# Layer 1's attention in a two-layer transformer kernel: projections cut in halves, transposes and softmax pieces moved between batches

## The chip, the cores and the metric

The kernel runs on one core of one Trainium2 chip, as one program with five instruction queues: TensorE (PE), VectorE (DVE), ScalarE (ACT), GpSimd (POOL) and SyncE (SP, which issues DMAs here). Each queue is executed in its own order, and semaphores tie them together. The metric is device time in microseconds; less is better.

## The reference, cut to what matters

Two layers run over x of 16 batches of 128 tokens, 128 wide. A layer is attention, then a feed-forward part. The change touches the first attention:

```
xn = layernorm(x) * g_norm                        # 16 batches x 128 tokens x 128
q  = l2norm((xn @ Wq) per head) * q_scale         # 16 heads of 64: 1024 columns
k, v = split(xn @ Wkv)                            # ONE key/value head of 64 for all 16 heads
k  = l2norm(k) * k_scale                          # null key and null value from cond_64 stand in front
sim = 8 * q @ k.T + relative position bias        # rel_pos_bias: a small MLP over distances
attn = softmax(causal and key mask(sim))          # 16 heads x 128 x 129
out = layernorm((attn @ v) @ Wout) * g_out
x  = x + ternary_ffn(out)                         # then layer 2: attention and an 8-expert top-2 MoE
```

The second attention has no l2norm of q and k; it ends in a router that chooses two of eight experts for every token, and those run last.

## The kernel before, in words

**Tiling.** One batch (128 tokens) is a step of a loop of 16. The 128 query rows of a batch are cut into four *units* u = 0..3 of 32 queries. A tile of scores has 128 partitions (4 head groups x 32 queries) and, for four such groups, 33, 65, 97 or 129 keys by unit: the causal mask lets later units see more keys. So a batch has four units of four pieces. Everything is fp32.

**The steps of a batch b, by their names in the code.** `input_norm` (DVE) normalises x; `turn_input` (PE) transposes it to psA, `input_T` (ACT) copies it out. `project_in` (PE, L761 to L777) multiplies it with Wkv (to psA) and with Wq in two halves h = 0, 1 of 512 columns (to the two banks of psQ). For the norm of q and k, `squares` (ACT, L1107 to L1113) squares both, `sum_squares` (DVE, L1416) adds up per head, POOL's `q_norm` (L584 to L590) takes a floor (L588) and a power -1/2 (L562), and `queries_norm` (DVE, L1421) multiplies. `turn_queries` (PE, L796) transposes the normed queries half by half back into psQ, `queries` (ACT, L1124) copies them to qT. `keys_in`, `turn_keys`, `keys_T` do the same for the keys.
Then, unit by unit: `scores` (PE, L810) to psS; `biased` (DVE, L1430) adds the bias that POOL's `mask_bias` (L613) has made and takes the row's maximum; `weights` (ACT, L1143) is the exponential with its sum; `divide` (DVE, L1438, L1442) normalises; `turn_pair` (units 0 and 1, L817) and `turn_probs` (units 2 and 3, L828) transpose; `pair_T` and `weights_T` (ACT, L1150, L1156) copy; `values_pair` and `values` (PE, L836, L846) multiply with v; `outputs` (DVE, L1451) reads; `project` (PE, L865) multiplies with Wout; `out_stats` and `out_centred` (DVE) start the output's norm. The value matrices of `values_pair` are spread to other partitions by six SP DMAs per batch (L478, L481), which wait for `values_set` (POOL, L596).

**What sets the order.** It is written out by hand: each engine's block has a function `batch(b, i)` that `over` calls, some first and last batches unrolled and the rest in a hardware loop of two. The two attentions share these functions, with `if layer == ...` where they differ. Work of neighbouring batches is interleaved: in batch b, PE also transposes and multiplies units 2 and 3 of b-1, projects Wout for b-2 and projects the input of b+2; ACT, DVE and POOL prepare q and k of b+1. psS has room for one unit of scores, so a unit's `scores` waits until DVE has read the one before; psQ holds both halves of one batch's q, so `project_in` of a batch waits until ACT has copied both transposed halves of the batch before (semaphore q_ready, raised once per batch).
POOL has one more duty in batches 3, 14 and 15 of the first layer: `hide` (L580) puts the causal mask into the second layer's bias table with 4, 6 and 6 instructions.

## Time and profile before

| | us |
|---|---|
| median of 3 runs | 679.77 (673.1, 679.77, 679.88) |
| the profiled execution's own time | 673.8 |
| its span | 672.1 |
| first attention, first scores to last projection | 55.8 to 278.9 |
| second attention's loop begins | about 336 |
| busy: PE, DVE, ACT, POOL | 493.2, 426.6, 378.4, 322.8 |

The span is what the profiler's records cover; the time adds what lies around it. Busy is the time in which an engine has an instruction in work; matmuls are pipelined and their ends are modelled. In a row of the timeline, the first number is the start from the span's beginning, the second the duration, and brackets tell how long the engine had been idle and on whose work it waited ("issue": for nothing that the profile shows). A line number is that of the kernel before.

### The profile page before, as it was taken

Reading aid. Unit: us, or ns where it says so; the run is one execution under the profiler, and the core shown is the slowest. Engines: PE = TensorE matmul, PEld = TensorE weight load, DVE = VectorE, ACT = ScalarE, POOL = GpSimd, SP = SyncE. Lnnn points to the kernel's source line nnn. Section 1 sums busy time; section 2 is a strip of 40 time slices with the busy share of each in tenths; the row PEclk is TensorE's granted clock in tenths of the full one; section 3 lists DMA queues with packets and bytes.
Section 4 is the critical chain, followed back from the end, with each engine's and each line's share of the span. In section 5 each row is a group of like instructions: output and inputs, shape, how many; then the busy total and the mean of one; then the engine's idle time right before and its main releaser. Section 6 shows DMA issues by size and latency. Waiting matters only on the chain.

```text
span 672.1 us, 13998 instructions
## 1 busy us (share of the span) xinstructions
PE 493.2 (73%) x3209; PEld 397.8 (59%) x3209; DVE 426.6 (63%) x2098; ACT 378.4 (56%) x1473; POOL 322.8 (48%) x397
## 2 busy tenths in 40 slices
PE   1057788888788887888679899999886505999930
PEld 0034566666566655756668787787775403887820
DVE  2644788778877888446367989888997421344313
ACT  1036876777677767465178787878685101444310
POOL 5235476446654683176343434252347660345660
PEclk9986999999999998999679999999999855999975
DMA  3822075220000000000000000000001112344316
GB/s 102 213 61 74 13 133 109 68 64 9 4 6 6 4 6 4 1 1 1 4 5 9 6 8 5 6 6 5 7 18 44 35 44 50 103 116 124 88 38 193
DMA packets 53757, 30.14 MB, mean 45 GB/s; under 512 B 19994, under 2 KB 50131, under 8 KB 53715
## 3 DMA queue, kind: packets, MB, share of 16 engines
q1 hardware_dynamic: 51154, 24.77, 15.7%
q0 software_dynamic: 2560, 4.90, 2.3%
q8 instruction: 15, 0.25, 0.2%
q14 instruction: 28, 0.22, 0.1%
HBM read 16.13 MB, written 11.42 MB: 41 GB/s over the span
## 4 chain that ended last, share of the span: by engine, by line
PE 39%; DVE 18%; issue 14%; SPq 10%; ACT 7%; DMA 6%; POOL 5%; DVEq 1%; POOLq 0%; ACTq 0%
PE psS L810 5%; PE psS L1061 5%; PE psQ L782 4%; DVE sc L1430 4%; DMA slot_rows<-Y,dest_u 4%; PE psQ L777 3%; PE psQ L1051 3%; PE psO L846 3%; ACT sc L1143 2%; SPq L448 2%; ACT qT L1124 2%; PE psA L865 2%; DVE centred L1494 2%; SPq L431 2%; DVE OT L1451 2%
## 5 line engine op out<-in xcount | busy, mean ns | idle before, releaser
L1143 ACT ACTIVATE sc<-sc,negmax 128x97 f32<-128x97 f32 (+3 forms) x512 | 179.2, 355 | 55.3 <-DVE negmax L1430 55.1
L1430 DVE CUSTOM_DVE_ANT_0 sc<-psS,wide_buf 128x97 f32<-128x97 f32 (+3 forms) x512 | 93.7, 239 | 65.2 <-PE psS L810 64.2
L810 PE MATMUL psS<-kk,qT 128*128 128x194 f32 (+3 forms) x512 | 102.7, 323 | 17.9 <-DVE negmax L1430 17.8
L613 POOL TENSOR_TENSOR wide_buf<-bias,mask 128x132 f32<-128x132 f32 (+3 forms) x128 | 104.3, 841 | 6.1 <-DVE negmax L1430 4.2
L810 PEld LDWEIGHTS psS<-kk,qT 128*128 128x128 f32 x512 | 81.1, 194 | 34.6 <-issue 30.7
L1143 ACT ACTIVATION_READ_ACCUMULATOR sc<-sc,negmax 128x1 f32 x512 | 97.8, 191 | 0.0
L1442 DVE TENSOR_TENSOR pn<-sc,rsum 128x128 f32<-128x128 f32 (+3 forms) x128 | 71.5, 559 | 8.7
L865 PE MATMUL psA<-Wo,OT 128*128 128x128 f32 (+1 forms) x512 | 65.5, 282 | 1.7 <-DVE OT L1451 1.7
L865 PEld LDWEIGHTS psA<-Wo,OT 128*128 128x128 f32 x512 | 62.9, 196 | 3.0 <-DVE OT L1451 2.6
L562 POOL TENSOR_TENSOR qrn<-qssc,half 128x9 f32<-128x9 f32 (+1 forms) x32 | 57.3, 1789 | 2.7
L588 POOL TENSOR_SCALAR qssc<-qss 128x9 f32<-128x9 f32 (+1 forms) x32 | 13.0, 405 | 91.8 <-DVE qss L1416 91.8
L1156 ACT COPY PT<-psT 96x512 f32<-96x512 f32 x64 | 37.4, 584 | 26.9 <-PE psT L828 26.0
L1451 DVE TENSOR_SCALAR OT<-psO,cols 128x512 f32<-128x512 f32 x64 | 47.7, 746 | 5.7 <-PE psO L846 3.9
L828 PE MATMUL psT<-ident,pn 128*96 128x128 f32 (+1 forms) x256 | 40.1, 280 | 14.8 <-issue 14.0
L1430 DVE DVE_READ_ACCUMULATOR2_ANT negmax<- 128x1 f32 x512 | 42.1, 82 | 0.0
L711 POOL DMA_INDIRECT choice_rows<-hT,tags x24 | 22.5, 939 | 39.7 <-ACT hT L1262 23.5
L828 PEld LDWEIGHTS psT<-ident,pn 128*96 128x96 f32 (+1 forms) x256 | 28.3, 140 | 19.9 <-issue 19.5
L846 PE MATMUL psO<-PT,vp 96*64 96x256 f32 (+1 forms) x256 | 34.8, 390 | 6.9 <-DVE OT L1451 5.3
L1061 PE MATMUL psS<-eW,hm 128*128 128x128 f32 x320 | 37.7, 277 | 2.7 <-DVE hm L1761 1.8
L625 POOL DMA_INDIRECT slot_rows<-Y,dest_u x32 | 31.3, 980 | 16.5 <-DMA slot_rows<-Y,dest_u 9.6
L1061 PEld LDWEIGHTS psS<-eW,hm 128*128 128x128 f32 x320 | 36.3, 192 | 4.8 <-issue 2.9
L596 POOL TENSOR_TENSOR vp<-kvs,vnull 128x64 f32<-128x64 f32 x32 | 13.1, 411 | 53.6 <-PE psO L846 53.6
(256 smaller groups left out, 1022.2 us busy)
## 6 DMA issues: line engine op xcount, KB each, us to landing
eW<-in_L_ffn_W SPq DMA_DIRECT2D x16, 256.0 KB, 3.0
slot_rows<-empty SPq DMA_DIRECT2D x2, 1390.0 KB, 11.7
xb<-slot_rows SPq DMA_DIRECT2D x16, 139.0 KB
vp_u<-vp SPq DMA_DIRECT2D x128, 8.0 KB
choice_rows<-zero_row SPq DMA_DIRECT2D x8, 256.0 KB, 3.0
wide_buf<-choice_rows SPq DMA_DIRECT2D x8, 256.0 KB, 4.5
Wq<-in_L_cond_Wq SPq DMA_DIRECT2D x2, 512.0 KB, 6.9
vp_u<-vp SPq DMA_DIRECT2D x64, 16.0 KB
```

The lines of the kernel that those rows point to most:

```text
L562: pool.tensor_tensor(dst, src, half[:, 0:k], ALU.pow).then_inc(done, count)
L613: pool.tensor_tensor(unit_masked(i, u).rearrange("p h e k -> p (h e) k"), unit_bias(layer, u).rearrange("p h e k -> p (h e) k"), mask[laye ...
L810: m = pe.matmul(psS[:, h, 0:2 * w], qT[i][:, h, u].rearrange("p m q -> p (m q)"), kk[i][:, :, 0:w], start=True, stop=True)
L828: m = pe.transpose(psT[0:k, probs_bank(u, i), g * P:(g + 1) * P], pn[u][:, g, :], ident[:])
L846: m = pe.matmul(psO[DH * e:DH * (e + 1), 2 * P * (u - 2):2 * P * (u - 1)], vp[i][0:k, :], PT[u - 1][0:k, :, e, :], start=True, stop=True)
L865: m = pe.matmul(psA[:, Y_AT[layer]:4 * P], OT[i][:, j].rearrange("p u q -> p (u q)"), Wo[layer][:, j, :], start=(j == 0), stop=(j == 7))
L1061: m = pe.matmul(psS[:, c, n * P:(n + 1) * P], hm[:, j, t * P:(t + 1) * P], eW2[i][:, j, :], start=(j == 0), stop=(j == FB - 1))
L1143: m = act.activation(v, v, ACT.Exp, bias=negmax[:, u, g:g + 1], scale=-1.0, accum_out=psum_row[:, u, g:g + 1])
L1156: act.copy(PT[u - 1][0:k].rearrange("p h e q -> p (h e q)"), psT[0:k, probs_bank(u, i), :]).then_inc(s["probsT_ready"], 1)
L1430: dve.tensor_tensor_reduce(sc[u][:, h, e, :], unit_psum(u)[:, h, e, :], unit_masked(i, u)[:, h, e, :], -1.0, -FAR, ALU.add, ALU.min, accum ...
L1442: dve.tensor_tensor(pn[u][:], sc[u][:].rearrange("p h e k -> p (h e) k")[:, :, 1:k + 1], rsum[:, u, :].unsqueeze(2).broadcast_to([P, 4, k] ...
L1451: dve.tensor_scalar(OT[i][:, :, 2 * half_of:2 * half_of + 2, :], psO[:].rearrange("p (u j q) -> p j u q", u=2, q=QB), cols[:, C_VN:C_VN + ...
```

## The change

The first layer's attention gets a function of its own on each engine (`attention_first`); the second layer's keeps the old order (`attention_second`). No arithmetic is added or taken away.

* **PE:** `project_in` is cut into `project_values` and `project_heads(b, h)`. The projection of b+1 (before: of b+2, at the end of b) now stands at the beginning of batch b: the k/v part and half 0 ahead of the first scores, half 1 behind them. `turn_queries` is cut as well: half 0 of b+1 comes at the end of batch b after its last scores, half 1 is the first thing of batch b+1. In the last batch's tail `project` of 14 goes ahead of `values_pair` of 15.
* **ACT:** q_ready rises per half. The copy of the queries (`queries`) moves to the beginning of their own batch; the exponentials of unit 3 of b-1, and their copy PT, move from the end of b-1 into batch b. `squares` is cut, its second half goes behind unit 0's exponentials.
* **DVE:** unit 3's `biased` of b-1 moves into batch b, with `divide` of unit 2. The statistics of the output are spread, so that none waits for the one just before it.
* **POOL:** floor and power of each half are apart from each other, with mask additions in between; the power of half 1 becomes the first instruction of the next batch. `values_set` of batch b moves from the end of b-1 to the beginning of b, and `hide` from the beginning of a batch to its end.
* **Second layer:** its two projection halves wait for q_ready one by one.

The core of the diff. The context is the new functions; lines that only moved into `attention_second` with `layer == 1` resolved are left out, and so are the removed lines, which the kernel above shows.

```diff
@@ POOL
+NORMS = ((0, 9), (9, HEADS + 1))
+def q_floored(b, h):
+    lo, hi = NORMS[h]
+    apart(pool, (s["ss_step"], 2 * b + h + 1))
+    pool.tensor_scalar(qssc[:, lo:hi], qss[:, lo:hi], 1e-24, None, ALU.max).then_inc(s["q_floor"], 1)
+def q_rsqrt(b, h):
+    lo, hi = NORMS[h]
+    pool.wait_ge(s["q_floor"], 2 * b + h + 1)
+    rsqrt(qrn[:, lo:hi], qssc[:, lo:hi], hi - lo, s["rn_ready"])
...
+def attention_first():
     def batch(b, i):
+        first, last = no(b, 0), no(b, NB - 1)
+        if not first:
+            q_rsqrt(b, 1)
+            values_set(0, b, i)
+        if not last:
+            mask_bias(0, b + 1, 0, 1 - i)
+            mask_bias(0, b + 1, 1, 1 - i)
+            q_floored(b + 1, 0)
+            mask_bias(0, b + 1, 2, 1 - i)
+            q_rsqrt(b + 1, 0)
+            mask_bias(0, b + 1, 3, 1 - i)
+            q_floored(b + 1, 1)
+        if isinstance(b, int) and b in (3, NB - 2, NB - 1):
             hide(b)
+    q_floored(0, 0)
+    q_rsqrt(0, 0)
+    q_floored(0, 1)
+    q_rsqrt(0, 1)
+    values_set(0, 0, 0)
+    pool.wait_ge(rel_in, 16 * 32)
+    pool.wait_ge(s["masks_ready"], 1)
+    for u in range(UNITS):
+        mask_bias(0, 0, u, 0)
+    over(pool, NB, batch, 4, 2)
+    for g in range(QUADS - 1):
+        dense_rstd(g)
...
@@ PE
+def project_values(b, i):
+    pe.wait_ge(s["xnT_ready"], b + 1)
+    held(pe, s["kk_ready"], b)
+    pe.matmul(psA[:, P:2 * P], xnT[i][:], Wkv[0][:], start=True, stop=True).then_inc(s["kv_psum"], 1)
+def project_heads(b, h, i):
+    held(pe, s["q_ready"], 2 * b + h - 1)
+    pe.matmul(psQ[:, h, :], xnT[i][:], Wq[0][:, 512 * h:512 * (h + 1)],
+              start=True, stop=True).then_inc(s["q_psum"], 1)
+def project_in(b, i):
+    B = b + NB
     pe.wait_ge(s["xnT_ready"], B + 1)
+    pe.matmul(psA[:, V_AT[1]:V_AT[1] + DH], xnT[i][:], Wkv[1][:, DH:P], start=True,
+              stop=True).then_inc(s["kv_psum"], 1)
+    pe.matmul(psA[:, KT_AT[1]:KT_AT[1] + P], Wkk[:].rearrange("p a d -> p (a d)"), xnT[i][:],
+              start=True, stop=True).then_inc(s["kT_psum"], 1)
+    if no(b, NB - 1):
         pe.wait_ge(s["r_pos_read"], 1)
+    for h in range(2):
+        pe.wait_ge(s["q_ready"], 2 * B + h - 1)
+        for j in range(4):
+            m = pe.matmul(psQ[:, h, j * P:(j + 1) * P], Wq[1][:, (4 * h + j) * P:(4 * h + j + 1) * P],
+                          xnT[i][:], start=True, stop=True)
+        m.then_inc(s["q_psum"], 1)
 def turn_keys(b, i):
     pe.wait_ge(s["k_ready"], b + 1)
     pe.transpose(psA[:, 2 * P:3 * P], kd[i][:].rearrange("p a d -> p (a d)"), ident[:]).then_inc(
         s["kT_psum"], 1)
+def turn_queries(b, h):
+    pe.wait_ge(s["qn_ready"], 2 * b + h + 1)
+    for j in range(4):
+        m = pe.transpose(psQ[:, h, j * P:(j + 1) * P], qn[:, (4 * h + j) * P:(4 * h + j + 1) * P],
+                         ident[:])
+    m.then_inc(s["qT_psum"], 1)
...
+def attention_first():
     def batch(b, i):
         first, last = no(b, 0), no(b, NB - 1)
+        turn_queries(b, 1)
+        if not last:
+            project_values(b + 1, 1 - i)
+            project_heads(b + 1, 0, 1 - i)
+        if not first:
+            turn_probs(b - 1, 2, 1 - i)
+        scores(0, b, 0, i)
+        if not first:
+            values_pair(b - 1, 1 - i)
+        if not last:
+            project_heads(b + 1, 1, 1 - i)
+        scores(0, b, 1, i)
+        if not first:
+            turn_probs(b - 1, 3, 1 - i)
+        if not first and not no(b, 1):
+            project(0, b - 2, i, not last)
+        scores(0, b, 2, i)
+        if not first:
+            values(b - 1, 1 - i)
+        scores(0, b, 3, i)
+        if not last and not no(b, NB - 2):
+            turn_input(0, b + 2, i)
+        if not last:
+            turn_keys(b + 1, 1 - i)
+            turn_queries(b + 1, 0)
+        turn_pair(b, i)
+    pe.wait_ge(attw_in, 16 * 8)
+    turn_input(0, 0, 0)
+    project_values(0, 0)
+    project_heads(0, 0, 0)
+    project_heads(0, 1, 0)
+    turn_input(0, 1, 1)
+    turn_keys(0, 0)
+    turn_queries(0, 0)
+    turn_ternary()
+    over(pe, NB, batch, 2, 2)
+    turn_probs(NB - 1, 2, 1)
+    project(0, NB - 2, 0, False)
+    values_pair(NB - 1, 1)
+    gate_rows_T()
+    turn_probs(NB - 1, 3, 1)
+    values(NB - 1, 1)
+    project(0, NB - 1, 1, False)
...
@@ ACT
+    if layer == 0:
+        held(act, s["kT_psum"], B)
     held(act, s["q_psum"], 2 * B - 2)
     c = C_GN0 if layer == 0 else C_GIN1
     act.activation(xnT[i][:], psA[:, 0:P], ACT.Copy, scale=cols[:, c:c + 1]).then_inc(
         s["xnT_ready"], 1)
+def squares(b, h):
     held(act, s["ss_step"], 2 * b)
+    if h == 0:
+        act.wait_ge(s["kv_psum"], b + 1)
+        act.activation(qsq[:, 0, :], psA[:, P:P + DH], ACT.Square)
+    act.wait_ge(s["q_psum"], 2 * b + h + 1)
+    act.activation(qsq[:, 1 + 8 * h:9 + 8 * h, :], psQ[:, h, :].rearrange("p (h d) -> p h d", d=DH),
+                   ACT.Square).then_inc(s["sq_ready"], 1)
 def queries(layer, b, i):
     B = b + NB * layer
             act.wait_ge(s["qT_psum"], 2 * b + h + 1)
         else:
             act.wait_ge(s["q_psum"], 2 * B + h + 1)
+        act.activation(qT[i][:, h].rearrange("p u m q -> p m u q"),
+                       psQ[:, h, :].rearrange("p (m u q) -> p m u q", u=UNITS, q=QB), ACT.Copy,
+                       scale=1.0 if layer == 0 else DH ** -0.5).then_inc(s["q_ready"], 1)
...
+def attention_first():
     def batch(b, i):
+        first, last = no(b, 0), no(b, NB - 1)
+        queries(0, b, i)
+        if not first:
+            pair_T(b - 1, 1 - i)
+        if not last:
+            squares(b + 1, 0)
+        if not first:
+            weights(4 * (b - 1) + 3, 3)
+            weights_T(b - 1, 2, 1 - i)
+        weights(4 * b, 0)
+        if not last:
+            squares(b + 1, 1)
+        if not first:
+            weights_T(b - 1, 3, 1 - i)
+        weights(4 * b + 1, 1)
+        weights(4 * b + 2, 2)
+        if not last and not no(b, NB - 2):
+            input_T(0, b + 2, i)
+        if not last:
+            keys_T(0, b + 1, 1 - i)
+    act.wait_ge(s["cols_ready"], 1)
+    input_T(0, 0, 0)
+    squares(0, 0)
+    squares(0, 1)
+    keys_T(0, 0, 0)
+    input_T(0, 1, 1)
+    ternary_T()
+    over(act, NB, batch, 2, 2)
+    pair_T(NB - 1, 1)
+    weights(4 * NB - 1, 3)
+    weights_T(NB - 1, 2, 1)
+    down_scaled()
+    gate_WoT()
+    weights_T(NB - 1, 3, 1)
...
@@ DVE
+def attention_first():
     def batch(b, i):
+        n = 4 * b
+        first, last = no(b, 0), no(b, NB - 1)
+        reads = not first and not no(b, 1)
+        queries_norm(b, 1)
+        if not first:
+            divide(b - 1, 2)
+        if reads:
+            outputs(b - 2, 1, i)
+        if not first:
+            biased(n - 1, 3, 1 - i)
+        if not last and not no(b, NB - 2):
+            input_norm(0, b + 2, i)
+        if not last:
+            sum_squares(b + 1, 0)
+            values_in(0, b + 1, 1 - i)
+        biased(n, 0, i)
+        if not first:
+            divide(b - 1, 3)
+            outputs(b - 1, 0, 1 - i)
+        biased(n + 1, 1, i)
+        divide(b, 0)
+        if not last:
+            queries_norm(b + 1, 0)
+            sum_squares(b + 1, 1)
+        else:
+            dense_stats(0)
+        if reads:
+            out_stats(0, b - 2, i)
+        biased(n + 2, 2, i)
+        if reads:
+            moments(b - 2, i)
+        if not last:
+            keys_in(b + 1, 1 - i)
+        else:
+            dense_stats(1)
+        if reads:
+            out_centred(b - 2, i)
+        divide(b, 1)
+    input_norm(0, 0, 0)
+    input_norm(0, 1, 1)
+    ternary()
+    values_in(0, 0, 0)
+    sum_squares(0, 0)
+    sum_squares(0, 1)
+    keys_in(0, 0)
+    queries_norm(0, 0)
+    over(dve, NB, batch, 4, 2)
+    divide(NB - 1, 2)
+    outputs(NB - 2, 1, 0)
+    biased(4 * NB - 1, 3, 1)
+    f_norm_in(0)
+    divide(NB - 1, 3)
+    outputs(NB - 1, 0, 1)
+    out_stats(0, NB - 2, 0)
+    moments(NB - 2, 0)
+    gate_rows_in()
+    out_centred(NB - 2, 0)
+    outputs(NB - 1, 1, 1)
+    f_norm_in(1)
+    dense_stats(2)
+    out_stats(0, NB - 1, 1)
+    moments(NB - 1, 1)
+    out_centred(NB - 1, 1)
...
```

The order on **PE** in a loop batch, before. The rows go from the last scores of a batch (L810, 258 columns) to the third piece of the next one:

```order
L796 MATMUL psQ<-ident,qn 128x128 x3
L340 ISA
L810 MATMUL psS<-kk,qT 128x258 [waits scores_ready,const_done]
L810 MATMUL psS<-kk,qT 128x258
L340 ISA
L817 MATMUL psT<-ident,pn 128x128 [waits probsT_ready,probs_ready,const_done]
L819 MATMUL psT<-ident,pn 128x128 x2
L767 MATMUL psA<-Wkv,xnT 128x128 [waits q_ready,xnT_ready]
L777 MATMUL psQ<-Wq,xnT 128x512 x2
L340 ISA
L810 MATMUL psS<-kk,qT 128x66 [waits q_ready,scores_ready,kk_ready,const_done]
```

and in the changed kernel, from the same place (L830 is `scores`, L816 `turn_queries`, L782 and L787 the projections, L848 `turn_probs`):

```order
L816 MATMUL psQ<-ident,qn 128x128 [waits qn_ready]
L816 MATMUL psQ<-ident,qn 128x128 x3
L782 MATMUL psA<-Wkv,xnT 128x128 [waits kk_ready,xnT_ready]
L787 MATMUL psQ<-Wq,xnT 128x512 [waits q_ready]
L848 MATMUL psT<-ident,pn 96x128 [waits probsT_ready,probs_ready,const_done]
L848 MATMUL psT<-ident,pn 96x128 x3
L340 ISA
L830 MATMUL psS<-kk,qT 128x66 [waits q_ready,scores_ready,kk_ready,const_done]
L830 MATMUL psS<-kk,qT 128x66
```

Between the last scores of a batch and the first of the next PE had both halves of the projection; now it has one half, the second half's transposes, and a piece of the batch before.

The order on **POOL** in batch 3, before (L613 `mask_bias`, L588 floor, L562 power, L596 `values_set`, L580 `hide`):

```order
L580 AFFINE_SELECT bias<-bias 32x4x32 x4
L613 TENSOR_TENSOR wide_buf<-bias,mask 128x132
L588 TENSOR_SCALAR qssc<-qss 128x9
L562 TENSOR_TENSOR qrn<-qssc,half 128x9
L588 TENSOR_SCALAR qssc<-qss 128x8
L562 TENSOR_TENSOR qrn<-qssc,half 128x8
L613 TENSOR_TENSOR wide_buf<-bias,mask 128x260
L613 TENSOR_TENSOR wide_buf<-bias,mask 128x388
L613 TENSOR_TENSOR wide_buf<-bias,mask 128x516
L596 TENSOR_TENSOR vp<-kvs,vnull 128x64
```

and in the changed kernel, batch 3 and the first instruction of batch 4 (L617 `mask_bias`, L589 floor, L600 `values_set`):

```order
L562 TENSOR_TENSOR qrn<-qssc,half 128x8
L600 TENSOR_TENSOR vp<-kvs,vnull 128x64
L617 TENSOR_TENSOR wide_buf<-bias,mask 128x132
L617 TENSOR_TENSOR wide_buf<-bias,mask 128x260
L589 TENSOR_SCALAR qssc<-qss 128x9
L617 TENSOR_TENSOR wide_buf<-bias,mask 128x388
L562 TENSOR_TENSOR qrn<-qssc,half 128x9
L617 TENSOR_TENSOR wide_buf<-bias,mask 128x516
L589 TENSOR_SCALAR qssc<-qss 128x8
L580 AFFINE_SELECT bias<-bias 32x4x32 x4
```

The power of half 1 now stands behind the batch's end, so in batches 3 and 14 `hide` stands between that half's floor and its power.

The order on **DVE** at the end of a loop batch in the changed kernel (L1508, L1512 `divide`, L1491 `queries_norm`, L1521 `outputs`, L1500 `biased`):

```order
L1512 TENSOR_TENSOR pn<-sc,rsum 128x256 [waits probsT_psum,rsum_ready]
L1491 TENSOR_TENSOR qn<-psQ,qrn 128x512 [waits qT_psum,rn_ready]
L1508 RECIPROCAL rsum<-psum_row 128x4 [waits exp_done]
L334 REGISTER_ALU [waits rsum_ready]
L1512 TENSOR_TENSOR pn<-sc,rsum 128x384 [waits probsT_psum]
L1518 REGISTER_ALU
L1521 TENSOR_SCALAR OT<-psO,cols 128x8x64 [waits out_psum]
L340 ISA
L1500 ISA sc,negmax<-psS,wide_buf 128x129 [waits bias_ready,scores_psum,probs_ready,const_done]
```

Before, `biased` of unit 3 (129 keys) stood directly behind the division of unit 1; now the second half's queries, a division and an output stand in between.

## Rows read from the trace of the kernel before

**Rows 1.** Chain of work that ended last, first layer's loop (start, us, what)
```profile
105.98 0.46 PE psA L767 x2
240.83 0.46 PE psA L767 x2
```

**Rows 2.** Busy time by stretch: ten batches of layer 1, then five of layer 2
```profile
core 0: us, PE busy (x) PEld busy (x) DVE busy (x) ACT busy (x) POOL busy (x), PEclk, DMA share, GB/s
106.00:240.83 134.83, 111.47 (x730) 85.69 (x731) 106.40 (x531) 100.25 (x431) 78.78 (x92) 1.00 0.11 28
390.60:448.20 57.60, 52.59 (x396) 46.00 (x395) 50.31 (x257) 46.09 (x202) 21.72 (x30) 1.00 0.03 6
```

**Rows 3.** Timeline of DVE, one batch of layer 1
```profile
172.88 0.29 DVE L1430 CUSTOM_DVE_ANT_0 sc<-psS,wide_buf 128x129 f32<-128x129 f32 x1 [1.12 <-PE psS L810]
176.25 0.20 DVE L1430 CUSTOM_DVE_ANT_0 sc<-psS,wide_buf 128x33 f32<-128x33 f32 x1 [0.99 <-PE psS L810]
```

**Rows 4.** Timeline of PE, the same batch
```profile
160.24 1.88 PE L777 MATMUL psQ<-Wq,xnT 128*128 128x512 f32 x4
171.18 0.66 PE L796 MATMUL psQ<-ident,qn 128*128 128x128 f32 x4 [0.38 <-DVE qn L1421]
173.50 0.46 PE L767 MATMUL psA<-Wkv,xnT 128*128 128x128 f32 x2 [0.46 <-ACT qT L1124]
```

**Rows 5.** Timeline of ACT, one batch
```profile
170.02 0.38 ACT L1143 ACTIVATE sc<-sc,negmax 128x97 f32<-128x97 f32 x1 [2.44 <-DVE negmax L1430]
```

**Rows 6.** Timeline of POOL, one batch
```profile
177.67 0.76 POOL L588 TENSOR_SCALAR qssc<-qss 128x9 f32<-128x9 f32 x1 [5.63 <-DVE qss L1416]
178.51 1.82 POOL L562 TENSOR_TENSOR qrn<-qssc,half 128x9 f32<-128x9 f32 x1
180.63 1.67 POOL L562 TENSOR_TENSOR qrn<-qssc,half 128x8 f32<-128x8 f32 x1
182.26 2.61 POOL L613 TENSOR_TENSOR wide_buf<-bias,mask 128x260 f32<-128x260 f32 x3
```

**Rows 7.** Timeline of PE in layer 2's loop: first scores of two batches, five apart
```profile
390.90 0.56 PE L810 MATMUL psS<-kk,qT 128*128 128x66 f32 x4
448.15 0.56 PE L810 MATMUL psS<-kk,qT 128*128 128x66 f32 x4
```

**Rows 8.** Groups by line and shape, layer 1 (busy us, mean ns | idle before)
```profile
L1421 DVE TENSOR_TENSOR qn<-psQ,qrn 128x512 f32<-128x512 f32 x25 | 17.1, 685 | 0.0
...
L1124 ACT ACTIVATE qT<-psQ 128x512 f32<-128x512 f32 x26 | 14.0, 594 | 0.0
```

**Rows 9.** Timeline of POOL: `hide` of batches 3 and 14
```profile
91.88 1.65 POOL L580 TENSOR_SCALAR_AFFINE_SELECT bias<-bias 32x128 f32<-32x128 f32 x4 [0.22 <-POOL vp L596]
...
239.46 3.52 POOL L580 TENSOR_SCALAR_AFFINE_SELECT bias<-bias 32x256 f32<-32x256 f32 x6 [0.20 <-issue]
```

**Rows 10.** Timeline of SP's DMA issues and of PE at the start
```profile
65.87 2.47 SPq L478 DMA_DIRECT2D vp_u<-vp  x4
70.98 0.68 PE L836 MATMUL psO<-PT,vp_u 128*128 128x128 f32 x4 [1.15 <-DMA vp_u<-vp]
```

**Rows 11.** Busy time by stretch, for the clock; columns as in Rows 2
```profile
66.00:67.00 1.00, 1.00 (x6) 1.00 (x5) 0.67 (x7) 0.17 (x1) 0.00 (x0) 0.50 0.21 57
```

**Rows 12.** Timeline of PE at the end of layer 1's attention
```profile
267.28 1.16 PE L836 MATMUL psO<-PT,vp_u 128*128 128x128 f32 x4
269.08 3.35 PE L865 MATMUL psA<-Wo,OT 128*128 128x128 f32 x16
278.75 0.60 PE L985 MATMUL psT<-ident,z 128*128 128x128 f32 x4
```

**Rows 13.** DMA issues on the page (KB each, median us to landing)
```profile
slot_rows<-empty SPq DMA_DIRECT2D x2, 1390.0 KB, 11.7
```

**Rows 14.** Groups by line and shape: layer 1, then layer 2 (busy us, mean ns)
```profile
L1442 DVE TENSOR_TENSOR pn<-sc,rsum 128x512 f32<-128x512 f32 x14 | 9.7, 692 | 1.0
...
L1442 DVE TENSOR_TENSOR pn<-sc,rsum 128x512 f32<-128x512 f32 x16 | 14.6, 914 | 0.9
L1494 DVE SCALAR_TENSOR_TENSOR centred<-Y,o_mv,g_out 128x128 f32<-128x128 f32 x14 | 15.0, 1073 | 0.0
```

More of the change, by code:

```diff
@@ L640, in batch, with attention_second @@
+            def attention_second():
+                def batch(b, i):
+                    if not no(b, NB - 1):
+                        for u in range(UNITS):
+                            mask_bias(1, b + 1, u, 1 - i)
+                        values_set(1, b + 1, 1 - i)
+                    if not (no(b, 0) or no(b, 1)):
                         output_rstd(b - 2, i)
-                    if layer == 1 and isinstance(b, int) and b >= NB - 3:
+                    if isinstance(b, int) and b >= NB - 3:
@@ L697, in _ @@
                     f_input_rstd(g - 1)
-            attention_in(1)
+            for u in range(UNITS):
+                mask_bias(1, 0, u, 0)
+            values_set(1, 0, 0)
             f_scale(QUADS - 1)
-            attention(1)
+            attention_second()
             for t in range(*GROUPS[2]):
@@ L974, in down_sums @@
                 m.then_inc(s["f_c_psum"], 1)
[L976 to L977 removed]
+            attention_first()
             def f_turn(g):
```

330 lines of the change are left out of this document (95 added, 235 removed).

## The prediction, made before the changed kernel was run

> **What bounds the kernel now.** I read the slices of the page first: none of the four engines is ever full in layer 1's attention, from 56 to 279 us. Then the chain of waits, which there jumps between PE, ACT, DVE and POOL: no engine is the bound, the order is. Two marks of the chain, ten batches apart, give the period: 240.83 - 105.98 = 134.85, so **13.49 us a batch** [rows 1]. The busy times of that stretch, by ten: PE 11.15, DVE 10.64, ACT 10.03, POOL 7.88 [rows 2]. Every batch loses 2.3 to 3.5 us on its busiest engines. The timelines show where. DVE waits twice a batch for scores, 1.12 and 0.99 us [rows 3]. The 1.12 comes because PE puts the last scores behind the second half's transposes, and these wait 0.38 for DVE's normed queries [rows 4]. The 0.99 comes because PE multiplies both projection halves, 1.88 us, before the next first scores [rows 4], while nothing is ready for DVE. ACT waits 2.44 us before unit 2's exponentials [rows 5], and POOL 5.63 us for the sums of squares [rows 6].
>
> **The change part by part.**
> *The loop.* No instruction goes; only idle time can. DVE's own queue is 10.64 us, PE's 11.15 (with modelled, overlapping ends), so no period is under about 11.0. I placed DVE's new queue beside the other three with the durations of the rows. The first scores now stand behind half a projection (0.94 of the 1.88) and DVE has unit 3's scoring of the batch before, a sum of squares and a copy of k and v to do meanwhile: the 0.99 is covered. The last scores stand ahead of all transposes, and DVE reads them only in the next batch: the 1.12 is covered by about 3 us of other work. ACT's 2.44 shrinks as unit 3's exponentials are done ahead of unit 0's. New hand-overs stay tight: the exponentials of unit 3 against `divide`, the copy of half 1 against the first scores, the power of half 1 against its `queries_norm`; each may show 0.1 to 0.3 us. That gives 11.0 + 0.2 to 0.5 = 11.2 to 11.5.
> The other end is a loop that exists. Layer 2 runs the same scores, exponentials and products: (448.15 - 390.90)/5 = 11.45 us a batch [rows 7], with PE 10.52 and DVE 10.06 busy, a fifth of 52.59 and 50.31 [rows 2]. It loses 0.9 on PE and 1.4 on DVE. Layer 1 with the same losses has 11.15 + 0.9 = 12.1, or 10.64 + 1.4 = 12.0. Between 11.2 and 12.1 I take **11.6**, a little nearer the placed queue because layer 2's order still has the late last scores that this change removes.
>
> *The ring through POOL.* Queries of half 1 go DVE, PE, ACT, then the next projection half, squares, sum, floor, power, and back. Its own pieces are 0.69 and 0.59 [rows 8], 0.66 [rows 4], 0.76 and 1.67 [rows 6], together 4.4; between copy and second squares stands about half of ACT's queue, 5. That is 9.4 with no hand-overs, some 10.2 with eight of 0.1: under 11.6, so it does not bind, with about 1.4 us to spare. Before, POOL ran both powers in one go after a 5.63 us wait, so its own queue (7.88) is no bound either.
>
> *`hide`.* It stands now between floor and power of half 1 in batches 3 and 14, so DVE's first step and PE's first transposes of batches 4 and 15 wait for it. It takes 1.65 + 0.22 and 3.52 + 0.20 [rows 9]; by my placing of the queues DVE has other work of 0.4 us left at that point. Cost 1.5 and 3.3 us, **4.8** together. Free before: it stood ahead of the first mask addition, and POOL had 5.63 idle there. Batch 15's `hide` runs beside the tail: nothing.
>
> *The start.* First scores come earlier, but that is worth nothing: `values_pair` of batch 0 waits for its spread values in both kernels. SP's issues for them begin at 65.87, behind the table loads, and PE could go at 70.98 after 1.15 us of idle [rows 10]. PE will now stand there some 3 us. The granted clock had just risen from 1.2 GHz, 0.50 between 66 and 67 us [rows 11], and may fall again in that idle: 0 to 2 us, I take 1.
>
> *The tail.* From `values_pair` of batch 15 at 267.28 to the feed-forward's first transposes at 278.75 are 11.5 us [rows 12]. `project` of 14, 3.35 us at half clock there, goes ahead of it. Whether the clock also stays up is open: gain 0 to 3.5, I take 1, which pays for the start.
>
> *The values' DMAs.* `values_set` comes about 3 us later in the order, and `values_pair` of a batch one batch later as before. Six issues of 0.62 us and a landing of 1.3 [rows 10] make 5 us; there are some 14 from one to the other (one period and 3 us). Covered. Behind a 1390 KB clear of batches 2 and 3, which lands after 11.7 us [rows 13] and was issued 7 us before, some 5 us more still fit.
>
> *The second layer's q_ready waits* fall on copies made half a batch earlier: nothing.
>
> *The sum.* Between 70.98 and 267.28 lie 196.3 us and fifteen steps. Now 15 x 11.6 + 4.8 = 178.8: **17.5 us less**. Start and tail cancel. All behind it moves up as it is, since nothing there hangs on an absolute time. The profiled execution took 673.8 (span 672.1 and 1.7 around it): 656.3. It lies with the lowest of the three runs; the median, 679.77, is 6.0 above it and two of three runs are there. Between 656.3 and 662.3 I say **659 us**.
>
> *A rule and a row.* The row: dividing 512 columns takes DVE 692 ns in layer 1 and 914 in layer 2, and a two-input operation on 128 columns takes 1073 there [rows 14], while 512 columns of another kind take 685 [rows 8]. So DVE is held up when POOL works beside certain operations, and in the new order POOL's mask additions (2.61 us for three [rows 6]) lie beside the divisions. My 11.6 has 0.1 to 0.2 for it, the difference of 0.22 in one of four divisions. The Trainium skill, page "SBUF — State Buffer", section "Who interferes with whom", says a DVE instruction with two SBUF inputs contends with a GpSimd instruction that reads SBUF, and that the loser is blocked until the other ends. By that rule a division that meets a mask addition waits for all that is left of it; the time would be between the first rival's 665 and the last's 698. The trace agrees in kind, with 914 against 692.
>
> **The rivals.**
> 1. *Losses as in layer 2 or worse* (16%): DVE is held up by POOL once or twice a batch, or a hand-over in the ring is late. For it: rows 14, and every engine is now near 90%. Period 12.2 to 12.6, 9 to 15 us given back: 665 to 673.
> 2. *Better than placed* (8%): all hand-overs fit, 11.0 to 11.1 a batch, clock stays up in the tail: 8 to 11 us more, 648 to 651.
> 3. *No change that can be told* (8%): the ring binds. That needs its spare 1.4 us and 1.2 more, from the floor and power at their slow values and each of the ring's DVE steps queued behind one late piece; period 12.8 to 13.4, 673 to 680. Against it: POOL has 3.7 us of idle a batch left to catch up.
> 4. *Slower* (6%): DVE and POOL take turns. A mask addition of each unit meets a two-input operation of DVE and is waited out whole: 2.61 + 0.6 for the first unit = 3.2 us a batch on DVE, 11.2 + 3.2 = 14.4, 0.9 over today's 13.49; over 15 steps 13.5 us, with `hide` 18: 698. It decides from the point at which DVE loses more than about 2 us a batch so. Against it: in layer 2 the four divisions lose only tenths.
> Could the change not do what it says? The order shows the halves apart on all four engines, so no.
>
> **How the numbers follow.** My forecast (periods 11.15 to 12.1, 652 to 666 with both levels of the runs) has 62%. About 1%, 6.8 us, is what a measurement of this kernel can tell from no change: faster is below 673. Forecast, rivals 1 and 2 make 86% faster; 8% the same; 6% slower. The range leaves rivals 3 and 4 and the ends of 1 and 2 out: 648 to 671.
>
> **What would show it.** In the trace after: first scores 11.2 to 12.1 us apart in layer 1's loop; DVE's waits for scores (1.12, 0.99) under 0.3 each; ACT's 2.44 under 1; POOL's wait for the sums of squares about 3; one step of about 13 us at batch 4 and one of about 15 at batch 15, with PE waiting for DVE's queries and these for POOL; `values_pair` of batch 0 again near 71, after 2 to 4 us of idle; layer 2's loop at 11.45. It is wrong if a wait of over 1 us stands in each batch, if the divisions take 0.9 us, or if the clock in the loop is under 1.00.

## The result, and the profile after

The changed kernel takes **658.08 us** (median of four runs, 655.63 to 659.76), the kernel before 679.83 beside it: ratio 0.970, 95% interval 0.963 to 0.977, faster. Forecast were 659 us and 648 to 671. The profiled execution took 659.76 us, 14 less than the 673.8 of before; its span is 658.0 against 672.1.

The first scores of each batch are the mark to read it by. Timeline of PE, layer 1 of the changed kernel (start, us, engine and line, what, idle before and its releaser):

```profile
64.70 0.56 PE L830 MATMUL psS<-kk,qT 128*128 128x66 f32 x4
84.62 0.63 PE L830 MATMUL psS<-kk,qT 128*128 128x66 f32 x4 [0.23 <-DVE negmax L1500]
...
109.30 0.63 PE L830 MATMUL psS<-kk,qT 128*128 128x66 f32 x4 [0.40 <-DVE negmax L1500]
...
132.31 0.63 PE L830 MATMUL psS<-kk,qT 128*128 128x66 f32 x4
...
240.40 1.09 PE L830 MATMUL psS<-kk,qT 128*128 128x66 f32 x4 [0.94 <-DVE negmax L1500]
```

From 132.31 the eighth next one comes at 225.38: (225.38 - 132.31)/8 = **11.63 us a batch**, where [rows 1] gave 13.49. Three steps are longer: 19.92 from batch 1 to 2 (64.70 to 84.62), 13.40 into batch 4 (95.90 to 109.30), 15.02 into batch 15 (225.38 to 240.40).

Busy time by stretch, changed kernel: those eight batches, the end of the first long step, and what follows the last; it answers to [rows 2] and [rows 11]:

```profile
132.31:225.38 93.07, 90.22 (x585) 69.37 (x585) 85.87 (x424) 80.21 (x345) 61.65 (x72) 1.00 0.07 17
66.00:68.00 2.00, 0.00 (x0) 0.00 (x0) 1.49 (x11) 2.00 (x12) 2.00 (x3) 1.00 0.25 69
68.00:70.00 2.00, 0.00 (x0) 0.00 (x0) 0.00 (x0) 0.29 (x2) 2.00 (x2) 0.84 0.09 16
70.00:76.00 6.00, 3.67 (x9) 2.48 (x10) 0.75 (x1) 0.00 (x0) 0.45 (x1) 0.50 0.10 18
240.00:247.00 7.00, 6.60 (x29) 6.45 (x30) 4.72 (x34) 5.03 (x26) 1.92 (x4) 0.51 0.04 8
```

PE is now busy for 97% of the loop and DVE for 92%, before 83 and 79%. The busy time is the same work (PE 11.28 a batch, before 11.15); the idle time went. The granted clock is full in the loop. From 57 us on it falls to half three times: in the idle time of PE at 65 to 72 us, behind the one at 235 to 238, and in the layer's tail (0.50 from 261 to 263 us).

The waits of [rows 3] are gone: in eight batches DVE waits for scores nowhere. ACT's wait ahead of unit 2's exponentials is 0.73 us, before 2.44 [rows 5], and POOL's for the sums of squares 3.38, before 5.63 [rows 6]. Timelines of ACT and POOL in one batch:

```profile
150.50 0.38 ACT L1195 ACTIVATE sc<-sc,negmax 128x97 f32<-128x97 f32 x1 [0.73 <-DVE negmax L1500]
```
```profile
145.19 0.26 POOL L589 TENSOR_SCALAR qssc<-qss 128x9 f32<-128x9 f32 x1 [3.38 <-DVE qss L1486]
```

What holds the loop at 11.63 is best seen in the chain of waits (start, us, what). Of the 11.64 us between two first projection halves (142.48 and 154.12) only this piece is not PE's, beside two of 0.1 to 0.2:

```profile
152.26 0.11 PE psA L776
152.37 0.12 PE psA L810
...
152.66 0.07 ACT xnT L1157
...
152.92 0.25 ACT kk L1188
...
153.18 0.07 ACT kk L1189
...
153.47 0.61 ACT qT L1177
154.08 0.04 issue
154.12 1.12 PE psQ L787 x2
```

PE turns the inputs and keys, ACT copies them and the first half of the queries, and only then may PE project the next batch over them: 1.63 us from 152.49 to 154.12. PE is busy meanwhile, with the other turns (152.31 to 154.1), but with nothing that the chain needs. So the busy share of 97% overstates PE's grip. A second way is nearly as tight: DVE's queries of half 1 end at 153.13 and PE turns them at 153.19.

### The profile page after: what moved, and what is told of

Same layout as the page of the kernel before. It is cut to its first block, busy times and chain, and to the rows that moved or that the text cites. A ratio compares the mean times of both kernels' runs of the same rounds, so it can differ in the third digit from the quotient of the medians.

```text
span 658.0 us, 14050 instructions
## 1 busy us (share of the span) xinstructions
PE 495.5 (75%) x3209; PEld 400.7 (61%) x3209; DVE 427.4 (65%) x2098; ACT 378.6 (58%) x1473; POOL 319.9 (49%) x397
## 4 chain that ended last, share of the span: by engine, by line
PE 47%; DVE 14%; issue 11%; SPq 10%; POOL 6%; DMA 6%; ACT 3%; DVEq 1%; POOLq 0%; ACTq 0%
PE psS L830 9%; PE psS L1112 5%; PE psA L885 5%; PE psQ L803 4%; PE psO L866 4%; PE psQ L787 4%; DMA slot_rows<-Y,dest_u 3%; DVE sc L1500 3%; PE psQ L1102 3%; SPq L448 2%; PE psT L848 2%; DVE centred L1561 2%; SPq L431 2%; DVE OT L1521 2%; POOL slot_rows L629 2%
## 5 line engine op out<-in xcount | busy, mean ns | idle before, releaser
L830 PE MATMUL psS<-kk,qT 128*128 128x194 f32 (+3 forms) x512 | 105.3, 328 | 20.9 <-DVE negmax L1500 19.5
L1500 DVE CUSTOM_DVE_ANT_0 sc<-psS,wide_buf 128x97 f32<-128x97 f32 (+3 forms) x512 | 93.0, 237 | 28.7 <-PE psS L830 26.9
L830 PEld LDWEIGHTS psS<-kk,qT 128*128 128x128 f32 x512 | 80.8, 196 | 46.1 <-issue 42.0
L617 POOL TENSOR_TENSOR wide_buf<-bias,mask 128x132 f32<-128x132 f32 (+3 forms) x128 | 103.0, 825 | 5.9 <-DVE negmax L1500 4.2
L1512 DVE TENSOR_TENSOR pn<-sc,rsum 128x128 f32<-128x128 f32 (+3 forms) x128 | 74.0, 578 | 8.2
L885 PE MATMUL psA<-Wo,OT 128*128 128x128 f32 (+1 forms) x512 | 67.6, 288 | 2.1 <-DVE OT L1521 2.1
L885 PEld LDWEIGHTS psA<-Wo,OT 128*128 128x128 f32 x512 | 64.7, 201 | 3.5 <-DVE OT L1521 3.3
L562 POOL TENSOR_TENSOR qrn<-qssc,half 128x9 f32<-128x9 f32 (+1 forms) x32 | 62.2, 1944 | 1.7 <-POOL bias L580 0.3
L1521 DVE TENSOR_SCALAR OT<-psO,cols 128x512 f32<-128x512 f32 x64 | 47.6, 743 | 11.0 <-PE psO L857 7.2
L589 POOL TENSOR_SCALAR qssc<-qss 128x9 f32<-128x9 f32 (+1 forms) x32 | 7.9, 248 | 80.4 <-DVE qss L1486 80.4
L848 PE MATMUL psT<-ident,pn 128*96 128x128 f32 (+1 forms) x256 | 40.1, 280 | 7.6 <-issue 6.6
L1500 DVE DVE_READ_ACCUMULATOR2_ANT negmax<- 128x1 f32 x512 | 41.6, 81 | 0.1
L848 PEld LDWEIGHTS psT<-ident,pn 128*96 128x96 f32 (+1 forms) x256 | 28.7, 138 | 20.0 <-issue 19.7
L629 POOL DMA_INDIRECT slot_rows<-Y,dest_u x32 | 31.3, 978 | 17.5 <-DMA slot_rows<-Y,dest_u 7.7
L600 POOL TENSOR_TENSOR vp<-kvs,vnull 128x64 f32<-128x64 f32 x32 | 12.4, 387 | 53.5 <-PE psO L866 53.5
```

The lines of the kernel that those rows point to most:

```text
L562: pool.tensor_tensor(dst, src, half[:, 0:k], ALU.pow).then_inc(done, count)
L617: pool.tensor_tensor(unit_masked(i, u).rearrange("p h e k -> p (h e) k"), unit_bias(layer, u).rearrange("p h e k -> p (h e) k"), mask[laye ...
L629: pool.indirect_dma_start(slot_d[c], bass.IndirectOffsetOnAxis(dest_u[:, t, c:c + 1], 0), Y[:, t, :], None).then_inc(s[f"slots_out{c}"], 16)
L830: m = pe.matmul(psS[:, h, 0:2 * w], qT[i][:, h, u].rearrange("p m q -> p (m q)"), kk[i][:, :, 0:w], start=True, stop=True)
L848: m = pe.transpose(psT[0:k, probs_bank(u, i), g * P:(g + 1) * P], pn[u][:, g, :], ident[:])
L885: m = pe.matmul(psA[:, Y_AT[layer]:4 * P], OT[i][:, j].rearrange("p u q -> p (u q)"), Wo[layer][:, j, :], start=(j == 0), stop=(j == 7))
```

## The experiments

Step times below are those of the first scores, read as above. The kernels ran on three chips, each beside the kernel before, which took 677.32, 676.85 and 677.33 us there. The changed kernel ran again on the first of them (`after_again`): ratio 0.9709 (0.9684 to 0.9734), 657.44 us, and the same steps to 0.02 us, but for the one at the start (19.25). Times below are compared with these 657.44 us.

> The changed kernel itself, as the reference for the kernels run beside it: 656 to 660 us, ratio 0.968 to 0.972 to the kernel before. Its layer 1 loop steps in 11.6 us, with three long steps: 19.9 us at the first batch, 13.4 at batch 4 and 15.0 at batch 15.

### The masking of the tables, and the spread values, earlier

`hide_early`, POOL's order, in attention_first:

```
                     if not first:
                         q_rsqrt(b, 1)
                         values_set(0, b, i)
+                        if isinstance(b, int) and b in (3, NB - 2, NB - 1):
+                            hide(b)
...
                     q_floored(b + 1, 1)
-                    if isinstance(b, int) and b in (3, NB - 2, NB - 1):
-                        hide(b)
```

> The masking of layer 2's bias tables (POOL, 4 instructions in batch 3, 6 each in batches 14 and 15) stands right behind the values of the same batch instead of at the batch's end. Theory 1, it is on the ring only because the next batch's second query scale is queued behind it, and POOL has an idle wait of 3.4 us further on that can take it: the steps of 13.4 and 15.0 us fall to 11.6 to 12, and the time by 4 to 5.5 us, to about 653. Rival, POOL has no free stretch on the way from there to the first query scale, or the masks come late to DVE's second unit: the loss only moves, and the time stays within 1.5 us.

651.16 us, ratio 0.9609 (0.9585 to 0.9632): 6.3 us under the changed kernel. That is a little more than the 4 to 5.5 expected. The steps of 13.40 and 15.02 became 11.67 and 12.37, a gain of 1.7 and 2.7; the step behind the first of them is 11.64 where it was 11.28, so that 1.4 are left of the 1.7. Timeline of POOL, first of the changed kernel, where the masking (L580) stands ahead of the power of half 1, then of this one:

```profile
102.31 1.70 POOL L580 TENSOR_SCALAR_AFFINE_SELECT bias<-bias 32x128 f32<-32x128 f32 x4
104.27 1.67 POOL L562 TENSOR_TENSOR qrn<-qssc,half 128x8 f32<-128x8 f32 x1 [0.27 <-POOL bias L580]
```
```profile
91.39 1.94 POOL L580 TENSOR_SCALAR_AFFINE_SELECT bias<-bias 32x128 f32<-32x128 f32 x4 [0.22 <-POOL vp L600]
93.42 1.04 POOL L617 TENSOR_TENSOR wide_buf<-bias,mask 128x132 f32<-128x132 f32 x2
95.61 0.25 POOL L589 TENSOR_SCALAR qssc<-qss 128x9 f32<-128x9 f32 x1 [1.16 <-DVE qss L1486]
```

The same work now comes out of POOL's wait for the sums of squares, 3.4 us elsewhere and 1.16 here. Further gain is the clock: here it is 1.00 from 230 to 250 us, and the step behind batch 15's first scores (234.73 to `values_pair` of batch 15 at 246.69) takes 11.96 us; in the changed kernel (240.40 to 255.00) 14.60, in `after_again` 14.54. About 1.4 us are given back in the tail, where the clock is 0.72 from 250 to 256 us: from `values_pair` of batch 15 to the feed-forward's first transposes are 8.72 us, in `after_again` 7.35. In the changed kernel the idle time on PE that ends so cost 2.6 us more than itself:

```profile
238.11 0.66 PE L816 MATMUL psQ<-ident,qn 128*128 128x128 f32 x4 [3.21 <-DVE qn L1491]
```

`values_early`, SP's order: the issues that spread batch 0's values stand ahead of layer 2's table loads, those of batch 1 in the middle.

```
+            spread_one(0, 0)
             for u in range(UNITS):
+                if u == 2:
+                    spread_one(1, 1)
                 (the 8 loads of a unit's table)
```

> SyncE sends the block-diagonal values of batch 0 ahead of the 32 table loads of layer 2 (16.9 us of issuing) and those of batch 1 in the middle of them. Theory 1, the 7.1 us that TensorE waits for them at 65 to 72 us are SyncE's queue alone: the wait goes, the clock doesn't fall behind it, the first step falls from 19.9 to 11.5 to 12.5 us, and the time by 7 to 8.5 us, to about 650. Rival, the transfers themselves are late (the 32 loads keep the DMA engines busy), or the wait goes to the tables that batch 3 masks: 2 to 4 us at most.

650.03 us, ratio 0.9619 (0.9586 to 0.9651): 7.4 us under the changed kernel by the medians, 6.1 by the ratios. Timeline of SP and of PE, changed kernel:

```profile
50.17 16.94 SPq L448 DMA_DIRECT2D bias<-in_fside_16xSxS  x32
67.22 2.47 SPq L478 DMA_DIRECT2D vp_u<-vp  x4
```
```profile
72.33 1.19 PE L856 MATMUL psO<-PT,vp_u 128*128 128x128 f32 x4 [7.08 <-DMA vp_u<-vp]
```

and with the edit:

```profile
49.43 2.99 SPq L447 DMA_DIRECT2D vp_u<-vp  x4
52.47 1.23 SPq L450 DMA_DIRECT2D vp_u<-vp  x2
53.74 7.96 SPq L460 DMA_DIRECT2D bias<-in_fside_16xSxS  x16
```
```profile
64.83 0.66 PE L863 MATMUL psO<-PT,vp_u 128*128 128x128 f32 x4
```

The transfers had not been slow: in the changed kernel the last of batch 0's six issues ends at 70.97 us, and PE starts 1.36 later. The queue ahead of them was, 32 issues of 0.53 us. The step of 19.92 became 11.48. Batch 0's own is 12.92 instead of 11.14: here the granted clock is 0.50 from 58 to 62 us, in the changed kernel 1.00. That is probably not this edit's doing, as `pe_plus` and `proj_whole`, below, have 12.83 and 12.65 there, also at half clock, without it. Both steps together take 24.40 us, in `after_again` 30.38.

`both_early` has both edits.

> Both of these edits. Theory 1: the two gains lie in different batches and add up, 11 to 14 us less than the changed kernel, 644 to 647 us. Rival: the tables now land so late that their masking, which now stands earlier in batch 3, waits for them (POOL's queue, with the query scales behind): less than the sum by 2 us or more.

644.38 us, ratio 0.9516 (0.9498 to 0.9535), 13.1 under the changed kernel where the two alone make 13.7: they add up within the spread of the runs, and these are two separate losses of the change.

### Parts undone

`proj_whole`: PE's `project_heads(b + 1, 1, 1 - i)` stands right behind half 0 again, ahead of the first scores.

> TensorE's second half of the query projection stands right behind the first again, ahead of the first scores: the same work, one stage of the order undone. Theory 1, TensorE bounds the loop by its own 11.2 us of work and the order of two of its stages costs only what becomes late: the first unit's scores come 0.9 us later, DVE waits for them for up to 0.9 us in a batch, of which its 1 us of idle time takes most: +0.2 to +0.6 us in each of 14 batches, 660 to 666 us. Rival A, DVE is the tight one (91% busy, no slack at the first scores): +0.9 in each, 670 us. Rival B, the halves do nothing: 657 us, no change.

654.44 us, ratio 0.9674 (0.9652 to 0.9695); the step is 11.68 against 11.63. Rival B held: in the loop the halves give 0.05 us a batch. Against the changed kernel's 0.9709 the intervals overlap, so the 3 us less are hardly told apart from nothing. The trace has the first scores of batch 2 at 82.15 us, `after_again` at 82.58, the step into batch 15 at 14.16 us against 15.01, and 1.9 us less from there to layer 2's first scores. Half of the 1.9 lies ahead of `values_pair` of batch 15, where the mean clock is 0.84 against 0.78; the rest stays open.

`unit3_dve`: DVE's scoring of the last unit back at its own batch's end. `unit3_both`: that, and ACT's exponentials too.

```
 DVE  divide(b, 1)
+DVE  biased(n + 3, 3, i)          (and gone from the next batch)
 ACT  keys_T(0, b + 1, 1 - i)
+ACT  weights(4 * b + 3, 3)        (unit3_both alone)
```

> Only DVE's share of that is undone (the bias and maximum of the last unit at the end of its own batch), ACT keeps the exponentials in the next batch. Theory 1, scaled queries of the second half end at 153.13 and TensorE's turns of them start at 153.19, so that 0.86 us ahead of them go straight on the path: +0.6 to +0.9 us in a batch, 666 to 671 us. Rival: TensorE fills the gap with the next projections, and the loop keeps 11.6: 657 us.

> The last unit's bias and maximum (DVE, 0.86 us) and its exponentials (ACT, 2.1 us) stand at the end of their own batch again, as in the kernel before. Theory 1: they then stand ahead of work that the next batch's first scores wait for. On DVE the second half of the scaled queries comes 0.9 us later, TensorE's second turns with it; ACT waits for the maximum at the end, and the squares of the second half, the weights' copies and the first unit's exponentials stand 2 us later: +0.8 to +1.5 us in a batch, 669 to 679 us. Rival: ACT has 1.5 us of idle time in a batch and DVE 1, and takes them up: +0.2 or less in a batch, 657 to 660 us.

`unit3_dve`: 665.77 us, ratio 0.9818 (0.9788 to 0.9848), steps of 12.17 and 12.31 in turn, from 133.42 to 231.23 us on average 12.23: +0.60. `unit3_both`: 684.49 us, ratio 1.010 (1.0065 to 1.0135), slower than the kernel before, by 1%; steps 13.3 to 14.4. Theory 1 held for the first, at the lower end of its range. For the second it held in kind, but 1.7 to 2.8 us a batch is more than the 0.8 to 1.5 that I gave it (669 to 679). In `unit3_dve` PE now waits where it didn't, timeline of PE:

```profile
155.92 0.66 PE L816 MATMUL psQ<-ident,qn 128*128 128x128 f32 x4 [0.96 <-DVE qn L1491]
```

In `unit3_both` DVE waits too, for squares that ACT makes behind the four exponentials (timeline of DVE):

```profile
153.68 0.75 DVE L1485 TENSOR_REDUCE qss<-qsq 128x9 f32<-128x576 f32 x1 [1.93 <-ACT qsq L1166]
```

`before_unit3` is the other way round: the kernel before, with this part alone.

```
 ACT  if layer == 0 and u == 0 and not first: weights(n - 1, 3)
 DVE  if layer == 0 and u == 0 and not first: biased(n - 1, 3, 1 - i)
      (both in front of unit 0, and gone from behind unit 2)
```

> The kernel before with one part of the change alone: the last unit's bias and maximum (DVE) and exponentials (ACT) stand at the start of the next batch; TensorE's and GpSimd's orders stay as before, with the turns of keys and queries behind unit 2 and the projections of batch b+2 at the end. Theory 1, this part alone made the gain (undoing it alone cost more than the whole of it): steps fall from 13.5 to 11.6 to 12.1 us and the time to 656 to 662 us. Rival, it needs the later turns and the projections near the first scores: DVE still waits for the second scale behind unit 2, the step falls by no more than 0.8 us, 665 to 675 us; and if ACT's copies of the queries now stand behind more, it doesn't fall at all, 677 us.

679.53 us, ratio 1.0028 (1.0005 to 1.0052): no gain, steps of 13.9 to 14.0 us, 0.45 longer than before. Timeline of DVE in its loop:

```profile
149.71 0.28 DVE L1435 CUSTOM_DVE_ANT_0 sc<-psS,wide_buf 128x129 f32<-128x129 f32 x1
152.05 0.19 DVE L1435 CUSTOM_DVE_ANT_0 sc<-psS,wide_buf 128x33 f32<-128x33 f32 x1 [2.05 <-PE psS L810]
```

DVE's wait of 1.12 for the last scores [rows 3] is gone, but the 0.99 for the first became 2.05: PE's order is the old one and has both projection halves in the way, and DVE's moved scoring only left it done sooner with nothing else. So the deferral is not the gain by itself: undone, it takes all of it, alone it gives none. It needs new orders of the other engines; which of them, no run here tells, as of the loop's other parts only the projection's halves were undone alone.

### One suspected bound at a time

`pe_plus`: `turn_queries(b + 1, 0)` issues its four transposes twice.

> TensorE turns the first half of the scaled queries twice (4 transposes of 128x128 more in each of 15 batches, 0.44 us by four at 0.11 us; the same result). Theory 1, TensorE bounds the loop: each step grows by 0.4 to 0.45 us, 6 to 6.5 us in all, 664 us. Rival, DVE's queue bounds it (112.9 of 124 us busy) and TensorE's 0.4 us of idle time in a batch take the work: +0 to +1.5 us in all, 657 to 659 us.

661.06 us, ratio 0.9757 (0.9730 to 0.9785). The steps did not move by 0.02 us (11.66, 11.62, 11.66, 11.63), though PE executed four more transposes in each (eight take 1.04 us where four take 0.60). The first scores of layer 2 start at 318.89, those of `after_again` at 319.31. The 3.6 us of its median come behind them, where both kernels have the same instructions, and I don't explain them. In layer 1 theory 1 fell, for this place in the batch: the extra transposes go into the 1.63 us in which the chain is on ACT. In the rest of the batch the chain lies on PE's own order, and no run put work there. Another order of ACT's five copies in that piece was not tried.

`nomask` leaves out layer 1's addition of the key mask (GpSimd's four additions a batch); DVE reads the tables themselves, and no longer waits for GpSimd there.

```
 def mask_bias(layer, b, u, i):
+    if layer == 0:
+        return
 ...
-    ... unit_masked(i, u)[:, h, e, :]
+    ... (unit_masked(i, u) if layer else unit_bias(0, u))[:, h, e, :]
```

> Layer 1's addition of the key mask to the bias tables is left out (GpSimd, 4 instructions a batch, 3.1 us; the output then ignores that layer's mask), DVE reads the tables themselves. Theory 1, DVE bounds the loop (TensorE took 0.44 us a batch more for nothing) and is slowed by GpSimd, which reads tables while DVE reads two SBUF operands: the divisions of 128x512 and 128x384 fall from 833 and 714 ns to 692 and 575, and the step by 0.2 to 0.45 us, 3 to 7 us in all, 651 to 654 us. Rival A, the divisions fall but the hand-over DVE, TensorE, ACT, DVE holds the loop: step 11.6, 656 to 658 us. Rival B, the divisions are slowed by something else: they stay at 0.8 us and the time stays.

654.42 us, ratio 0.9672 (0.9629 to 0.9715), step 11.50 on average. Groups of DVE by shape between 96 and 220 us (busy us, mean ns | idle before), the changed kernel and then this one:

```profile
L1512 DVE TENSOR_TENSOR pn<-sc,rsum 128x512 f32<-128x512 f32 x11 | 9.3, 845 | 0.4
L1512 DVE TENSOR_TENSOR pn<-sc,rsum 128x384 f32<-128x384 f32 x10 | 7.0, 696 | 1.3
```
```profile
L1515 DVE TENSOR_TENSOR pn<-sc,rsum 128x512 f32<-128x512 f32 x11 | 7.6, 692 | 0.4
L1515 DVE TENSOR_TENSOR pn<-sc,rsum 128x384 f32<-128x384 f32 x11 | 6.1, 558 | 1.3
```

The mask additions do slow the divisions, by 0.15 and 0.14 us on average. Of 0.29 us a batch the step gave back 0.13. PE's turns of unit 3 start 0.11 us behind the end of the division of 128x512 (146.84 and 146.95), and the idle time before them falls from 1.9 us to 0.9 over eleven batches; the chain passes there, and not through the other division. It lies between theory 1 and rival A. So neither the theory that PE bounds the loop nor the one that DVE does holds as it stands. As I read the chain, it is PE's order plus ACT's hand-over plus a short wait for a division; of these, only the division's part was changed in a run and moved the step.

`pow2`: one more power of 8 columns (1.67 us) on POOL ahead of that of half 1.

> GpSimd computes one more power of 8 columns (1.67 us) ahead of the scale of the second half, in 15 batches, with nobody reading it. Theory 1, from the prediction: the ring through GpSimd has 1.4 us to spare, the step grows by 0 to 0.3 us, to 657 to 662 us. Rival, from the changed kernel's trace, where the second scale ends at 152.13 us and DVE's multiplication by it starts at 152.44: DVE's queue waits for it at once, all but 0.3 us of it is on the path, the step grows by 1.3 us to 12.9 to 13.0, and the time to 676 to 678 us.

675.03 us, ratio 0.9963 (0.9943 to 0.9983); the step is 12.87, so 1.24 of the 1.67 is on the path. Timelines of POOL and DVE:

```profile
142.56 1.67 POOL L596 TENSOR_TENSOR pow_d<-qssc,half 128x8 f32<-128x8 f32 x1
144.19 1.71 POOL L563 TENSOR_TENSOR qrn<-qssc,half 128x8 f32<-128x8 f32 x1
```
```profile
145.93 0.69 DVE L1494 TENSOR_TENSOR qn<-psQ,qrn 128x512 f32<-128x512 f32 x1 [1.52 <-POOL qrn L563]
```

The ring through POOL is 12.87 - 1.67 = **11.2 us**, and its spare 0.43. The theory from my prediction fell; the rival held but for the last tenth (12.9 to 13.0 and 676 to 678 us were expected).

`both_whole` has both early edits and the whole projection.

> The version that the runs point to: the masking of the tables and the block-diagonal values early (644.4 us together), and the second half of the projection whole behind the first (ratio 0.9674 against 0.9709). Theory 1, the whole projection's gain was at the start, where TensorE had more to do ahead of its wait, and that wait is gone: 643 to 646 us, no difference to the two edits alone. Rival, it lies in the end of the layer and adds up: 641 to 643 us.

645.72 us, ratio 0.9512 (0.9468 to 0.9557), against 0.9516 of `both_early`: no difference. So if `proj_whole` won anything, it is not won on top of these two. The best that was tried is 644 to 646 us, and these two kernels cannot be told apart.

## Why the prediction was right

**The period, right.** Forecast 11.6, measured 11.63. Both waits of DVE are covered, ACT's 2.44 is 0.73 (I said under 1), POOL's 5.63 is 3.38 (about 3). But what I named as its grounds holds only in part: of the first scores I said that half a projection before them instead of a whole one helps; `proj_whole` puts that at 0.05 us a batch. Cover is enough, and without the deferred unit it is gone (`unit3_dve`, `unit3_both`).

**The ring through POOL, wrong in size.** I had 9.4 to 10.2 us and 1.4 to spare; `pow2` gives 11.2 and 0.43. What I left out is above all a wait in DVE's queue: in one batch of the changed kernel ACT's squares of half 1 end at 147.96 us and DVE sums them at 149.26, behind a scoring, a division and the other half's product. These 1.3 us on my 9.4 to 10.2 make 10.7 to 11.5, but in part by luck, as other terms were off both ways: the squares and the sum itself (0.58 and 0.68) had no time in my sum, while the floor takes 0.24 us and not 0.76 (in the kernel before it stood beside a division), and between the copy and the squares are 4.5 us and not 5. The ring did not bind, so the sum came out; with one late piece more, rival 3 would have come.

**`hide`, right.** 1.5 and 3.3 us were forecast; the steps are 1.8 and 3.4 longer than 11.63 (13.40 and 15.02), and moving it took 1.7 and 2.7 of that away. The step behind the first makes up 0.35 of it (11.28).

**The start, right in kind.** `values_pair` of batch 0 came at 72.33 us, 1.35 later than before [rows 10], where I took 1. The idle before it is 7.08 us, not 3: PE was there earlier than I placed it. That costs nothing by itself, but the clock fell to 0.50 between 70 and 76 us.

**The tail, half right.** From `values_pair` of batch 15 (255.00) to the feed-forward's first transposes (263.99) are 8.99 us, before 11.47 [rows 12]: 2.5 less, in the range of 0 to 3.5 and above the 1 that I took. Whether the clock stays up decides it, as I had left open: here it fell to 0.50 from 261 to 263 us, and in `after_again`, where it is 1.00 throughout, the same stretch takes 7.35 us, 4.1 less than before.

**The sum.** I had 178.8 us between the two `values_pair` and found 255.00 - 72.33 = 182.67. The thirteen steps between the first scores of batches 2 and 15 are as forecast: 240.40 - 84.62 = 155.78 against 13 x 11.6 + 4.8 = 155.6. The missing 3.9 are the two ends: 12.29 instead of 11.6 before them, and 14.60 instead of 11.6 behind, 3.0 us, nearly all of it at half clock. That I had not seen: I priced `hide` of batch 14 by the time that PE waits, and not by what the clock does after 3.21 us of it. In all the changed span is 14.1 us shorter, not 17.5. The forecast of 659 held because two misses cancel: the profiled execution is 3.5 us above my 656.3, but the median lies 1.7 under it, where that of before lay 6.0 above its own. That it came within a microsecond is luck.

**Layer 2, right.** From 376.15 to 444.88 us are six batches of 11.46, forecast 11.45 [rows 7].

**The rivals.** Rival 1's losses stand in layer 1 as 0.15 us in a division, not 0.6 to 1 a batch. Rival 4 would have had the divisions wait out whole mask additions. The Trainium skill, page "SBUF — State Buffer", section "Who interferes with whom", has the loser of such a pair blocked until the other ends. For a division that starts beside a mask addition the trace agrees. Timelines of POOL and DVE, changed kernel:

```profile
145.40 0.90 POOL L617 TENSOR_TENSOR wide_buf<-bias,mask 128x388 f32<-128x388 f32 x1
152.41 1.05 POOL L617 TENSOR_TENSOR wide_buf<-bias,mask 128x132 f32<-128x132 f32 x2
164.05 1.05 POOL L617 TENSOR_TENSOR wide_buf<-bias,mask 128x132 f32<-128x132 f32 x2
```
```profile
146.02 0.82 DVE L1512 TENSOR_TENSOR pn<-sc,rsum 128x512 f32<-128x512 f32 x1
153.36 0.56 DVE L1512 TENSOR_TENSOR pn<-sc,rsum 128x384 f32<-128x384 f32 x1
164.72 0.79 DVE L1512 TENSOR_TENSOR pn<-sc,rsum 128x384 f32<-128x384 f32 x1
```

When the first division starts, 0.28 us of the additions are left, and it takes 0.13 us longer than the 0.69 of `nomask`. At the third, 0.38 are left, and it takes 0.23 longer than the 0.56 of `nomask`; at the second only 0.10 are left, and it takes its 0.56. The longest division of 128x512 between 96 and 220 us takes 1.02 us and has 0.47 left of an addition at its start. Each time the loss is what was left of the addition, less 0.14 us. So rival 4's mechanism is in the kernel, and what failed of it is that whole additions would meet a division: most of the addition has run when the division starts. For the power the rule does not come out: in `nomask` each division of 128x512 starts 0.49 us into POOL's power of 1.83 us, which reads SBUF too, and takes 0.69 us as if alone.
